# Attention scores with keys on partitions, and fp32 probabilities weighed one step later

## The reference

```
q = rope(layernorm(x) @ wq)                      # 8 batches, 56 queries, 32 heads x 128
k = rope(ctx @ wk);  v = ctx @ wv                # 1500 keys, 8 heads x 128, each used by 4 query heads
attn = softmax(q @ k.T / sqrt(128) + mask)       # over the 1500 keys
x = x + tanh(g_xattn) * (attn @ v) @ wo
x = x + tanh(g_ffn) * lora_experts(layernorm(x)) # top 2 of 4 experts, rank 16
```

## Time and profile before

| | us |
|---|---|
| median of 3 runs | 2008.79 (2007.59 to 2008.92) |
| profiled execution, from its first to its last instruction | 2005.4 |
| PE busy | 1976.7 (99%), 12404 matmuls |
| DVE busy | 1235.0 (62%) |
| ACT busy | 1034.3 (52%) |
| POOL busy | 311.6 (16%) |

### The profile page before, as it was taken

The page is one execution under the profiler, slowest core; times in us unless marked ns, Lnnn a source line. Parts: engine busy times, 40 slices in busy tenths (PEclk is TensorE's granted clock), DMA queues, the critical chain, the costliest instruction groups (busy, mean ns, idle before and its releaser), DMA issues. The chain is left out here.

```text
span 2005.4 us, 32965 instructions
## 1 busy us (share of the span) xinstructions
PE 1976.7 (99%) x12404; PEld 1775.9 (89%) x12404; DVE 1235.0 (62%) x2639; ACT 1034.3 (52%) x1754; POOL 311.6 (16%) x227
## 2 busy tenths in 40 slices
PE   7999999999999999999999999999999999999998
PEld 7989889988899988998899988998899998999786
DVE  6766556666666666666666666666665666566544
ACT  6655555554545555555644555455554555455532
POOL 5511111111111111111111111111111111111200
PEclk9999999999999999999999999999999999999998
DMA  7611212111211212221111112221111112121270
GB/s 227 248 56 35 35 18 44 35 31 20 43 10 33 36 17 44 35 35 20 39 19 25 35 20 41 36 35 20 39 25 26 28 20 41 36 33 15 48 263 19
DMA packets 74904, 94.41 MB, mean 47 GB/s; under 512 B 22692, under 2 KB 49444, under 8 KB 74760
## 3 DMA queue, kind: packets, MB, share of 16 engines
q1 hardware_dynamic: 73752, 86.01, 20.4%
q10 hardware_dynamic: 1008, 6.42, 0.8%
HBM read 76.64 MB, written 15.77 MB: 46 GB/s over the span
## 5 line engine op out<-in xcount | busy, mean ns | idle before, releaser
L673 POOL TENSOR_TENSOR k_lo<-k_work,k_hi 128x500 fp32r<-128x500 f32 x192 | 244.1, 1285 | 1541.0 <-ACT k_hi L720 1513.3
L821 PE MATMUL low_banks<-wv_hi,cT_hi 128*125 128x256 f32 x1536 | 443.1, 288 | 0.0
L821 PE MATMUL low_banks<-wv_hi,cT_lo 128*125 128x256 f32 x1536 | 431.0, 281 | 0.0
L821 PE MATMUL low_banks<-wv_lo,cT_hi 128*125 128x256 f32 x1536 | 430.9, 281 | 0.0
L1027 DVE TENSOR_TENSOR pT<-t_banks,pT 125x448 fp32r<-125x448 f32 x384 | 236.0, 622 | 242.8 <-ACT pT L785 242.8
L1002 DVE CUSTOM_DVE_ANT_0 prob<-low_banks,mask_t 112x500 f32<-112x500 f32 x384 | 259.1, 678 | 178.2 <-PE low_banks L845 176.9
L785 ACT ACTIVATE pT<-t_banks 125x448 fp32r<-125x448 f32 x384 | 205.1, 543 | 309.2 <-PE t_banks L857 308.2
L760 ACT ACTIVATE prob<-prob,neg_max 112x1500 f32<-112x1500 f32 x128 | 198.6, 1552 | 289.7 <-DVE neg_max L1007 288.9
L805 PE MATMUL low_banks<-cT_hi,wk_hi 128*128 128x500 f32 x768 | 312.0, 406 | 0.0
L805 PE MATMUL low_banks<-cT_hi,wk_lo 128*128 128x500 f32 x768 | 298.6, 389 | 0.0
L805 PE MATMUL low_banks<-cT_lo,wk_hi 128*128 128x500 f32 x768 | 298.3, 388 | 0.0
(11 more groups left out here) (136 smaller groups left out, 2910.2 us busy)
## 6 DMA issues: line engine op xcount, KB each, us to landing
stage<-in_ctx_dram SPq DMA_DIRECT2D x72, 250.0 KB
attn_by_head<-attn SPq DMA_DIRECT2D x65, 112.0 KB, 1.7
wq_raw<-in_L_xattn_wq_dram SPq DMA_DIRECT2D x7, 1024.0 KB, 7.2
q_raw<-q_by_head SPq DMA_DIRECT2D x64, 112.0 KB, 4.9
inv_b<-inv_by_head SPq DMA_DIRECT2D x64, 112.0 KB, 5.1
head_rows<-in_ctx_dram SPq DMA_DIRECT2D x24, 250.0 KB
mask_t<-in_mask_BxSxS_ff_dram SPq DMA_DIRECT2D x16, 328.1 KB
stage<-in_L_xattn_wo_dram SPq DMA_DIRECT2D x4, 1024.0 KB, 7.3
```

The lines of the kernel that those rows point to most:

```text
L673: nc.gpsimd.tensor_tensor(k[1][:, c * SC:(c + 1) * SC], k_rot[:, s], f32(k[0][:, c * SC:(c + 1) * SC]), ALU.subtract).then_inc(k_lo, 1)
L821: mm = nc.tensor.matmul(sv_banks[0:ST, m % 2, t * PAIR:(t + 1) * PAIR], cT[a][:, d, tile * ST:(tile + 1) * ST], w[1][mv][:, d, g * DH:g * ...
```

## The change

- Scores are made with keys on partitions (`k` tile of 125 keys stationary, the 224 queries moved), two tiles of keys in one bank of the `t_banks` ring. The transposes of the probabilities go away.
- The mask is turned once per batch (`B`, 6 transposes) into `mask_keys`; DVE adds it from there (`mask`).
- The maximum over keys is now across partitions: DVE takes it over the 12 tiles of each partition in two instructions (`max0` over 8 tiles, `max1` over 4 and the first result), PE turns the result (`MT`), DVE reduces it to one number per query (`rows`), PE turns that back spread over all partitions (`MB`), and DVE subtracts it, from PSUM, from the weights in three instructions of 4 tiles (`sub`). ACT takes the exponent in three instructions (`exp`).
- Probabilities and values stay whole fp32: one fp32 matmul per key tile in place of two fp32r ones, no splitting on ACT or DVE. It is done one step later (a `z` before a task: of the step before), so weights and values have two buffers.
- The sums over keys: POOL adds up the tiles (`add`, `total`), one fp32 matmul with ones (`SUM`) spreads them over all partitions, DVE inverts 128 x 224 numbers and multiplies. The way over DRAM goes away.
- Cosine products are written in place in PSUM; POOL has an order of its own, unrolled; SP stores the output after its other loads of the step.

```diff
 PE_STEP = {
-    "even": ("K00 S0 S1 K01 K02 S2 S3 K03 K10 S4 S5 K11 K12 K13 V40 K20 T0 T1 K21 V41 K22 T2 K23 PV0 V50 T3 PV1 T4 "
-             "V51 PV2 T5 PV3 PV4 PV5"),
...
-    "last": "S0 S1 S2 S3 S4 S5 O0 T0 T1 T2 PV0 T3 PV1 T4 PV2 T5 PV3 PV4 PV5 O1",
+    "odd": ("S0 zPV0 S1 S2 zPV1 S3 S4 zPV2 zPV3 zPV4 K00 K01 S5 K02 K03 K10 zPV5 zSUM K11 MT K12 K13 MB V00 V01 "
+             "V10 K20 K21 K22 K23 V11 V20 V21"),
+    "even": ("zPV0 S0 S1 zPV1 S2 zPV2 S3 S4 zPV3 K00 zPV4 zPV5 S5 zSUM K01 K02 K03 MT K10 K11 K12 MB V30 K13 V31 "
+             "V40 K20 K21 K22 K23 V41 V50 V51"),
+    "turn": ("S0 S1 zPV0 S2 S3 zPV1 C0 S4 C1 zPV2 zPV3 S5 zPV4 C2 C3 zPV5 zSUM B0 B1 K00 C4 K01 K02 K03 MT C5 C6 "
+             "V00 MB C7 V01 C8 C9 K10 K11 K12 C10 C11 V10 V11 K13 K20 K21 K22 K23 V20 V21"),
+    "last": ("S0 S1 zPV0 S2 zPV1 S3 zPV2 S4 zPV3 S5 zPV4 zPV5 zSUM O00 MT O01 MB O02 O03 PV0 PV1 PV2 PV3 PV4 PV5 "
+             "O10 O11 SUM O12 O13"),
...
 DVE_STEP = {
+    "even": ("mask0 mask1 mask2 mask3 max0 mask4 mask5 max1 rows sub0 cos0 sin0 rot0 sub1 Q sin1 zinv znorm sub2 "
+             "cos1 rot1 cos2 sin2 rot2"),
+    "turn": ("mask0 mask1 mask2 mask3 C0 mask4 max0 C1 mask5 C2 C3 B0 B1 max1 C4 zinv znorm rows C5 C6 cos0 C7 "
+             "sin0 rot0 C8 C9 sub0 sub1 C10 C11 sub2 Q cos1 sin1 rot1 cos2 sin2 rot2"),
...
+POOL_STEP = {
+    "even": "add1 add2 add3 klo0 klo1 klo2 add4 add5 total",
+    "pre_last": "add1 add2 klo0 klo1 klo2 add3 add4 add5 total wo0 wo1 wo2 wo3",
+    "last": "attn0 attn1 attn2 attn3 add1 add2 add3 add4 add5 total",
...
-        def scores(b, g, i):
...
+        def scores(b, g, j, last):
...
+            for t in range(2):
+                tile = slice((2 * j + t) * ST, (2 * j + t + 1) * ST)
+                for n, (a, m) in enumerate(PASSES):
+                    mm = nc.tensor.matmul(t_banks[0:ST, item % 2, t * GQ:(t + 1) * GQ], k[a][:, tile], q[m][:, :],
+                                          start=(n == 0), stop=(n == len(PASSES) - 1))
+            mm.then_inc(t_ready, 1)
...
+        def turn_max(n):
...
+            for h in range(HALVES):
+                mm = nc.tensor.transpose(m_bank[0:ROWS, h * ST:(h + 1) * ST], key_max[:, h * ROWS:(h + 1) * ROWS], ident[0:ST, 0:ST])
...
+        def spread_max(n):
...
+            for h in range(HALVES):
+                mm = nc.tensor.transpose(m_bank[0:ST, h * ROWS:(h + 1) * ROWS], row_max[:, h:h + 1].broadcast_to([ROWS, ST]),
+                                         ident[0:ROWS, 0:ROWS])
...
+            nc.tensor.matmul(sums_b, ones[:, :], tile_sum[:, :], start=True, stop=True, skip_group_check=True).then_inc(sums_spread, 1)
...
+        def weigh(n, j):
...
+            probs = pair_weights(n, j)
             for t in range(2):
+                mm = nc.tensor.matmul(o_acc, v[n // 2 % 2][:, 2 * j + t, (n % 2) * DH:(n % 2 + 1) * DH], probs[:, t],
+                                      start=(j == 0 and t == 0), stop=(j == PT - 1 and t == 1), skip_group_check=True)
...
+        def add_mask(b, g, j, last):
...
+            nc.vector.tensor_tensor(pair_weights(n, j).rearrange(four, h=REP),
+                                    t_banks[0:ST, item % 2, 0:2 * GQ].rearrange("p t (h s) -> p t h s", t=2, h=REP),
+                                    mask_keys[:, j, :, None, :].broadcast_to([ST, 2, REP, SQ]), ALU.add).then_inc(t_free, 1)
+
+        def max_begin(b, g, last):
...
+            nc.vector.tensor_reduce(weights[:, NT, :], pair_weights(b * HKV + g, 0, SHIFTED).rearrange("p t q -> p q t"),
+                                    AX_X, ALU.max).then_inc(max_begun, 1)
...
+        def shift(n, j):
...
+            group = pair_weights(n, j * GROUP, GROUP)
+            nc.vector.tensor_tensor(group, group, max_b[:, None, :].broadcast_to([ST, 2 * GROUP, GQ]), ALU.subtract).then_inc(p_shifted, 1)
...
+            nc.vector.reciprocal(inv_b[:, :], sums_b).then_inc(inv_ready, 1)
```

More of the change, by code:

```diff
@@ L139, in k_item, with t_item, v_item, next_pair @@
     return b * K_ITEMS + g * NC + c
[L142 to L159, removed]
+def t_item(b, g, what, n, last=False):
+    return b * T_ITEMS + (T_FIRST + g * PT + t_place(step_kind(g, last), what, n))
+def v_item(pair, m):
+    return pair * VT + m
+def next_pair(step):
+    return (step + step % 2) // 2
 def wait_apart(eng, sem, value, passed):
@@ L583, in c_tile, with pair_weights @@
         return shared.c_slots[m % STAGE_RING]
+    def pair_weights(n, j, count=1):
+        first = 2 * j if n % 2 == 0 else NT + 1 + 2 * ((j + PT - SHIFTED) % PT)
+        return weights[:, first:first + 2 * count, :]
     store_last_queries, query_sync, query_gpsimd, query_scalar, query_tensor, query_vector = query
@@ L687, in attn_low_head, with step @@
             low.then_inc(shared.attn_lo if h == REP - 1 else pieces, 1)
-        def batch(b, last):
-            for g in range(1, HKV + 1 - last):
-                for c in range(NC):
-                    if last and g == HKV - 1 and c == 1:
-                        pool.wait_ge(shared.wo_hi, 1)
-                        for h in range(REP):
-                            wo_low_head(h)
-                    k_low(k_item(b, g, c), (g * NC + c) % 2, c)
-        with pool.Fori(0, B - 1) as b:
-            batch(b, False)
-        batch(B - 1, True)
-        pool.wait_ge(shared.attn_hi, 1)
-        for h in range(REP):
-            attn_low_head(h)
+        def step(b, g, last):
+            for what, ago, (j, *_) in tasks(POOL_STEP[step_kind(g, last)]):
+                n = b * HKV + g - ago
+                if n < 0:
+                    continue
+                if what == "add":
+                    pool.wait_ge(p_exp, n * GROUPS + (j // GROUP + 1))
+                    if j == 1:
+                        so_far = pair_weights(n, 0)
+                        if n:
+                            pool.wait_ge(sum_ready, n)
+                    else:
+                        so_far = key_sum[:, :, :]
+                        pool.wait_ge(p_added, n * ADDS + (j - 1))
+                    nc.gpsimd.tensor_tensor(key_sum[:, :, :], so_far, pair_weights(n, j), ALU.add).then_inc(p_added, 1)
+                if what == "total":
+                    pool.wait_ge(p_added, n * ADDS + ADDS)
+                    if n:
+                        pool.wait_ge(sums_spread, n)
+                    nc.gpsimd.tensor_tensor(tile_sum[:, :], key_sum[:, 0], key_sum[:, 1], ALU.add).then_inc(sum_ready, 1)
+                if what == "klo":
+                    k_low(k_item(b, g + 1, j), ((g + 1) * NC + j) % 2, j)
+                if what == "wo":
+                    if j == 0:
+                        pool.wait_ge(shared.wo_hi, 1)
+                    wo_low_head(j)
+                if what == "attn":
+                    if j == 0:
+                        pool.wait_ge(shared.attn_hi, 1)
+                    attn_low_head(j)
+        for b in range(B - 1):
+            for g in range(HKV):
+                step(b, g, False)
+        for g in range(HKV):
+            step(B - 1, g, True)
     @block.scalar
@@ L747, in _ @@
             if what == "V":
-                v_high(n, n)
+                v_high(0, n)
         def step(b, g, last):
             kn = k_item(b, g + 1)
-            kind = step_kind(g, last)
-            for what, (n, *_) in tasks(ACT_STEP[act_kind(g, last)]):
-                s = ((g + 1) * NC + n) % 2
-                if what in ("C", "T"):
-                    t_bank = t_place(kind, what, n) % 2
+            for what, ago, (j, *_) in tasks(ACT_STEP[step_kind(g, last)]):
+                n = b * HKV + g - ago
+                if n < 0:
+                    continue
+                s = ((g + 1) * NC + j) % 2
@@ new lines, in scores @@
+        def scores(b, g, j, last):
+            item = t_item(b, g, "S", j, last)
+            if j == 0:
+                pe.wait_ge(q_lo, b * HKV + (g + 1))
+            pe.wait_ge(t_free, item + 1)
+            pe.wait_ge(k_lo, k_item(b, g, 2 * j // CT) + 1)
+            for t in range(2):
+                tile = slice((2 * j + t) * ST, (2 * j + t + 1) * ST)
+                for n, (a, m) in enumerate(PASSES):
+                    mm = nc.tensor.matmul(t_banks[0:ST, item % 2, t * GQ:(t + 1) * GQ], k[a][:, tile], q[m][:, :],
+                                          start=(n == 0), stop=(n == len(PASSES) - 1))
+            mm.then_inc(t_ready, 1)
@@ L880, in _ @@
         query_tensor(pe, c_transposes)
         pe.wait_ge(shared.w_lo, HKV)
-        for what, n in tasks(PE_STEP["first"]):
+        for what, ago, n in tasks(PE_STEP["first"]):
             if what == "V" and n[0] < RING and n[1] == 0:
@@ L1178, in _ @@
         with sp.Fori(1, pairs - 1) as i:
-            output_loads(sp, shared, wo, attn_dram, i, sp_passed)
+            for u in range(2):
+                output_load(sp, shared, wo, attn_dram, i, u, sp_passed)
         for t in range(NTT):
@@ L1375, in flamingo_block @@
         with ExitStack() as ctx:
[L1376 removed]
```

(1 more changed line is left out.)

448 lines of the change are left out of this document (231 added, 217 removed), and 51 rows, old and new, of tables (ACT_STEP, DVE_STEP, PE_STEP, POOL_STEP).

## The result

The changed kernel takes 1973.2 us (median of 4 runs, 1971.75 to 1974.67), beside 2008.7 for the kernel before (4 runs, 2007.59 to 2008.92). The ratio is 0.9825, with a 95% interval of 0.9811 to 0.9839. Faster was forecast, by 49 us; 36 came. The time lies in the range (1936 to 1998), 13 us above the point. The profiled run took 1971.75 us, its span is 1970.0.

What follows compares the result with a forecast made beforehand. PE, busy for 1976.7 of 2005.4 us, was taken to bound the kernel. PE's list -67, turn +10 and last step +6 gave -51, 1954 profiled; the median 3.4 above, 1958; handovers 2, 1960. Range 1936 to 1998.

Steps and rivals of the forecast that it cites:

- PE's list: PE's matmuls in each step: 9.5 us in place of 10.6, -1.05 a step, -67 us over 64 steps.
- The scores: 36 fp32r matmuls a step on PE at 0.111 us each, read as a weight-load floor: 4.0 us (3.8 to 4.3).
- The price of whole fp32: Weighing on PE: 24 fp32 records a step at 0.19, 4.6 us, dearer than two fp32r matmuls by 0.8.
- Rival (b): PE's matmul prices at their upper ends: 10.3 against 10.6 us a step, 2006, no change; chance 0.06.
- The turn: Step that turns the mask: C1 waits for C0's bank, about 1.0, and 0.4 more at B1; +10 us.
- rival (a): DVE's maximum over strided keys: at twice the price an element MT is late, 7.2 a batch, 2018; chance 0.10.
- DVE's price list: DVE's new work in a step: max0 2.0, max1 1.3, mask 0.62 each, inverse 0.4; 18 us of 27 with keys.
- The slack before MT: Even step: PE has 6.8 us of work before MT, DVE needs 5.2 for the maximum; holds by 1.5.
- The reciprocal: DVE's inverse of 224 elements: 0.4 us by the slope, up to 2.0, no row of that size.
- rival (d): Queues late by half a microsecond each step (slow reciprocal, POOL and DVE in each other's way): 1990; chance 0.13.
- (e): POOL becomes late for the keys, k_lo some 4 late in three steps of a batch: 2055; chance 0.04.
- The last step: O00 waits 8.5 us for POOL, O10 1.3, group 2 0.5, lower clock 1.8: 12 lost against 6, +6 us.

Runs made afterwards that it cites:

- With neighbours: Changed kernel with its two maximum reductions reading the same numbers as neighbours, not 896 bytes apart (maximum over keys left out): 1949.0 us, ratio 0.9707.
- one rounded pass: Changed kernel weighing values in a single fp32r pass, low halves left out: 1892.0 us; with the maximum reductions over neighbours as well, 1786.1 us.
- the small additions: Changed kernel with POOL's additions and total over 8 of 224 columns, the other sums left out: 1962.1 us, ratio 0.9772.

## Why the prediction was right and wrong

**PE's list** (-1.05 a step, 215.8 a batch) held, and gave up a little more than forecast. With neighbours a batch takes 215.8 all told, and of it 0.75 is the wait of the turn and 0.7 the two gaps at the score banks. That leaves 214.3, 0.2 a step better than forecast. The scores are at 0.11, as taken, and halving their columns changed nothing, so a floor that does not go by the moved columns was read rightly; that it is the weight load stays open. The price of whole fp32 came out near: 2.6 to 2.9 a step against one rounded pass, where the prediction's prices give 24 x 0.19 - 12 x 0.11 = 3.2. No row of before shows the 0.19 taken for an fp32 record of 224 columns; in the changed kernel eight of them start at 887.90, the next matmul starts at 889.25 and has 0.15 over its like behind it, which is 0.19 for each. Rival (b) is out.

**The turn** was forecast at 1.4 a batch. In the changed kernel the listed waits are 1.5 a turn, and 0.75 are left once the maximum is short. So C1's wait for the bank of C0 was seen rightly in kind, at half its size. The other half is C2 behind max0, which rival (a) had.

**The step that failed is DVE's price list**: "max0 over 1792 elements 2.0, max1 over 1120 1.3". They take 3.35 and 2.15, because each output reads elements 896 bytes apart; read as neighbours, the same two take 2.02 and 1.32. That is rival (a) in mechanism, at 1.71 times the price an element, just under the 1.8 from which I let it decide. The slack before MT was worked out well: the reductions are 2.2 longer, the slack was 1.5, so MT had to be 0.7 late; PE loses 0.78 there, twice a batch. So it cost 3.0 a batch, and not the 7.2 worked out for twice the price. Why a read at that distance costs more, no run shows: groups of 4, 5 and 8 take 1.77 and 1.78 ns an element, groups of 3 at the same stride 1.15. The rival should have had more than one chance in ten: that all rows of before have one slope says nothing of a pattern that none of them reads.

**The reciprocal** was put at 0.4, with 2.0 as upper end; it is 1.55. I had it behind cover everywhere, and it is not: it makes DVE late at the start of two steps, and costs 1.03 a batch, 8 us (11 by the times, with the last step's clock). That is rival (d) at a small size.

**How a batch adds up.** 217.2 was forecast; PE's list takes 1.5 less and C1 and B1 0.65 less, the stride costs 2.95, and the two gaps at the score banks 0.7: 218.7. So the time came out nearer to the forecast than its parts: two errors in DVE's prices and two the other way cancel in part, and that is luck.

**DVE and POOL** (part of (d), and (e)): POOL is late for no key beyond 0.2 us. But its additions slow the DVE instructions with two inputs in SBUF (859 and 693 ns, for 749 and 390 with the small ones), and stand ahead of O00's operands; together that is most of the 11 us that the small additions gave. **The last step**: O00 8.0 for 8.5, O10 1.8 for 1.3; right. The wait for the next head group is 1.9 for 0.5, and the matmuls at the lower clock cost 3.5 for 1.8 (a granted clock of 0.50; eleven behind O00's wait, nine behind this one), so 15 were lost where 12 were forecast. Some 6 to 8 us of it come back by another order on POOL.

## What to carry to other kernels

When a change turns a layout, price each reduction by the distance between the elements it now reads (at 896 bytes 1.78 ns an element here, for 1.04); if no row has such a pattern, measure it first, and else fold with tensor_tensor over whole tiles, but not while POOL works: there they took about twice as long here (1.59 and 1.43 us, for 0.86 and 0.64). A queue at 78% isn't covered because its sum fits: work out where each step's first instruction on it lands, since the two-bank ring passed on 0.35 and 0.37 us here. And small gaps of PE (starts 0.37 apart for 0.12) are not in the list of waits: lay the starts of two kernels side by side.

## What the runs showed of the hardware

- tensor_reduce over fp32 at a stride of 896 bytes costs 1.77 to 1.78 ns an element for groups of 4, 5 and 8, against 1.04 for neighbours, but only 1.15 for groups of 3 (925 ns for 672 elements). Why, I can't tell; no run varied the stride.
- The reciprocal of 224 elements from PSUM takes 1546 ns, a copy of them 379.
- DVE's tensor_tensor slows beside a busy POOL if both inputs lie in SBUF (POOL busy for 38% against 21%: 859 against 749 ns for 500 elements, 693 against 390 for 224), while those with one input in PSUM keep their time (676 and 679, L1059 622). With POOL at work all through the maximum of the last step, four of its five tensor_tensor of 448 elements take 1.43 to 1.59 us. A tensor_reduce from SBUF, with its one input, keeps its time (3346 and 3352 ns with the small additions and the whole ones). In single instructions of the changed kernel: L1005 at 772.18 has POOL's addition beside it until 772.63 and takes 0.98 us; L1005 at 774.91 takes 0.67, and POOL's k_lo, which starts beside it at 775.00, takes 1.70; the k_lo at 767.57, beside DVE instructions with an input in PSUM, takes 1.26.
